# Cross-attention, two layers, one core: rounded spread product, weighted sums two by two, last item behind two shifted steps

## What is computed

```python
# layer 0: queries from x, keys and values from ctx and x together (512 keys)
h = concatenate([ctx, x], axis=1)
q = x @ q_w + q_b;  kmat, v = split(h @ kv_w + kv_b)
attn = softmax(where(mask, q @ kmat.T / DH, -inf))
y = (attn @ v) @ out_w + out_b + x
x1 = gelu(rmsnorm(y) @ w1 + b1) @ w2 + b2 + x
# layer 1: queries from x1, keys and values from the normed ctx (256 keys)
a = layer_norm(ctx);  Q, K, V = x1 @ Wq.T, a @ Wk.T, a @ Wv.T
out = x1 + tanh(gate) * (softmax(Q @ K.T * DH**-0.5) @ V) @ Wo.T
```

## Time and profile before

| what | value |
|---|---|
| median of 3 runs | 2582.08 us (2581.36 to 2582.22) |
| span of the profiled execution | 2577.6 us |
| layer 0's batches | from 52 to 1130 us, 67.3 us each |
| MLP | from about 1140 to 1840 us |
| layer 1's batches | from about 1870 to 2577 us, 43.07 us each |
| PE's granted clock, mean | 0.980 of 2.4 GHz |

### The profile page before, as it was taken

One profiled execution on the slowest core, in us unless ns is written; L12 is line 12 of the kernel. 1 busy time (PEld: TensorE's weight loads), 2 busy tenths in 40 slices (PEclk: granted clock), 3 DMA queues, 4 the chain that ended last, 5 costly groups with the idle time before them and its releaser, 6 DMA issues. The chain is left out here.

```text
span 2577.6 us, 43920 instructions
## 1 busy us (share of the span) xinstructions
PE 2485.2 (96%) x14784; PEld 1931.8 (75%) x14784; DVE 1163.7 (45%) x2222; ACT 1497.8 (58%) x3418; POOL 226.3 (9%) x256
## 2 busy tenths in 40 slices
PE   6999999999999999989999999999899999999998
PEld 5677777777777777658888888888778787877775
DVE  4455555555555555542222122112356565656563
ACT  3777777777777777753222222222267676767675
POOL 1000000000000000010000000000221111121210
PEclk8999999999999999889999999999899999999998
DMA  6433343333444443341111011002244444444442
GB/s 171 100 99 99 98 102 98 97 98 99 106 107 107 107 107 91 91 127 67 50 49 48 1 49 49 30 19 81 82 115 125 121 125 120 126 120 126 119 111 75
DMA packets 148186, 239.00 MB, mean 93 GB/s; under 512 B 25600, under 2 KB 59680, under 8 KB 148144
## 3 DMA queue, kind: packets, MB, share of 16 engines
q1 hardware_dynamic: 148144, 238.46, 34.4%
HBM read 86.28 MB, written 25.21 MB: 43 GB/s over the span
## 5 line engine op out<-in xcount | busy, mean ns | idle before, releaser
L529 ACT ACTIVATE l_score_ps<-l_score_ps,l_neg_max 128x512 f32<-128x512 f32 (+1 forms) x1024 | 567.1, 557 | 291.3 <-DVE l_neg_max L705 289.3
L705 DVE TENSOR_REDUCE l_neg_max<-l_score_ps 128x1 f32<-128x512 f32 (+1 forms) x768 | 490.0, 682 | 69.5 <-PE l_score_ps L942 69.5
L549 ACT ACTIVATE l_probs<-l_score_ps 128x1024 f32<-128x1024 f32 x384 | 386.8, 1018 | 91.8 <-PE l_score_ps L975 89.1
L1239 ACT ACTIVATE mlp_hidden<-mlp_hidden_ps,mlp_b_col 128x512 f32<-128x512 f32 x128 | 88.3, 690 | 495.9 <-PE mlp_hidden_ps L66 495.8
L942 PE MATMUL l_score_ps<-l_stack 97*128 97x512 f32 (+1 forms) x1024 | 319.0, 370 | 27.4 <-ACT l_score_ps L529 12.8
L1274 DVE TENSOR_TENSOR mlp_hidden_l<-mlp_hidden,mlp_hidden_h 128x512 fp32r<-128x512 f32 x128 | 92.9, 725 | 519.3 <-ACT mlp_hidden_h L1241 519.3
L975 PEld LDWEIGHTS l_score_ps<-l_stack 99*128 99x128 f32 x1536 | 211.2, 192 | 116.8 <-issue 90.8
L975 PE MATMUL l_score_ps<-l_stack 99*128 99x256 f32 x1536 | 274.7, 305 | 0.0
L990 PE MATMUL l_o_ps<-l_probs,l_v 128*32 128x256 f32 x3072 | 241.2, 394 | 1.8
L721 DVE TENSOR_TENSOR l_o_norm<-l_o_ps,norm_room 128x256 f32<-128x256 f32 x128 | 54.4, 425 | 387.9 <-PE l_o_ps L990 387.9
L942 PEld LDWEIGHTS l_score_ps<-l_stack 97*128 97x128 f32 x1024 | 175.3, 193 | 71.3 <-ACT l_score_ps L529 40.5
(11 more groups left out here) (133 smaller groups left out, 4308.6 us busy)
## 6 DMA issues: line engine op xcount, KB each, us to landing
l_stack<-room SPq DMA_DIRECT2D x256, 192.0 KB
l_stack<-l_qk SPq DMA_DIRECT2D x256, 128.0 KB
l_stack<-room SPq DMA_DIRECT2D x128, 128.0 KB
l_stack<-l_qk SPq DMA_DIRECT2D x256, 64.0 KB
l_tokens<-in_x SPq DMA_DIRECT2D x16, 512.0 KB, 4.1
l_tokens<-in_ctx SPq DMA_DIRECT2D x16, 512.0 KB, 5.0
l_stack<-room SPq DMA_DIRECT2D x128, 64.0 KB
l_rows<-in_x SPq DMA_DIRECT2D x16, 512.0 KB, 3.4
```

Source lines behind the costliest of these rows:

```text
L529: m = act.activation(e, e, ACT.Exp, bias=neg_max[:, q, h:h + 1], accum_out=row_sum[:, q, h:h + 1])
L549: act.activation(probs[:, s % PROBS, :].rearrange("p (a b) -> p a b", a=2), score_ps[:, 2 * (s % 2):2 * (s % 2) + 2, :], ACT.Exp).then_inc ...
L705: dve.tensor_reduce(out, bank, AXIS_X, ALU.max, negate=True).then_inc(max_done, 1)
L1239: act.activation(hidden[:, m % HBUF, :], hidden_ps[m % 4][:, :], ACT.Gelu_apprx_tanh, bias=b1_col[:, m:m + 1])
```

## The change

Three things, in both layers.

1. The spread becomes a rounded product over the whole array: `shiftT` and `spread` have 128 rows (zeros below) and are float32r; the reciprocal sums are held in a high and a low part (`INV_ROW`, `INV_LOW_ROW`), both of which `spread` picks up. `make_shift` has two more small operations on DVE, `turn_shift` turns 32 columns in place of 24. The set-up on POOL fills two larger tiles and selects twice.
2. The second pass goes by two steps: two shifted, two weigh, with PROBS = 4 and the projections behind the pair.
3. `shifted(a, 0)`, `shifted(a, 1)` and `turn_shift(a, 1)` stand ahead of the last item on PE, and on ACT `exps(a, 0)`, `copy_shift(a, 1)` and `exps(a, 1)` ahead of that item's `high`. The wait for `low_done` stays ahead of the loop. SP's stacks of half 0 wait for at least LOW_WAITED = 5 shifted steps: 5 in place of 4 in layer 1, no change in layer 0.

The DMA scratch of the program is set to 8192, which makes room.

```diff
-    PROBS = 3
+    PROBS = 4
+    LOW_WAITED = 5
...
-    SHIFT_ROWS = INV_ROW + HALF
+    INV_LOW_ROW = INV_ROW + HALF
+    SHIFT_ROWS = INV_LOW_ROW + HALF
...
-        shiftT = sb("shiftT", [SHIFT_ROWS, HALVES, S])
+        inv_raw = sb("inv_raw", [P, QT, HALF])
+        shiftT = sb("shiftT", [P, HALVES, S], F32R)
...
-        spread = sb("spread", [SHIFT_ROWS, GROUPS, P])
+        spread = sb("spread", [P, GROUPS, P], F32R)
...
-                            sp.wait_ge(shifted_done, PSTEPS * a + PSTEPS // HALVES * (half + 1))
+                            sp.wait_ge(shifted_done, PSTEPS * a + max(PSTEPS // HALVES * (half + 1), LOW_WAITED))
...
             def iteration(p, a):
                 for slot in range(SLOTS + 1):
+                    if slot == SLOTS and a is not None:
+                        exps(a, 0)
+                        copy_shift(a, HALVES - 1)
+                        exps(a, 1)
...
                 if a is not None:
-                    for s in range(PSTEPS):
+                    copy_inv(a, 1)
+                    for s in range(2, PSTEPS):
                         exps(a, s)
-                        if s == 1:
-                            copy_inv(a, 1)
...
                 dve.tensor_copy(high.bitcast(F32R), src).then_inc(shift_step, 1)
-                dve.reciprocal(shift[:, half, :, INV_ROW:SHIFT_ROWS], row_sum[:, :, heads])
-                dve.wait_ge(shift_step, HALVES * a + half + 1)
-                dve.tensor_tensor(shift[:, half, :, HALF:2 * HALF].bitcast(F32R), src, high, ALU.subtract
-                                  ).then_inc(shift_made, 1)
+                dve.reciprocal(inv_raw[:, :, :], row_sum[:, :, heads]).then_inc(shift_step, 1)
+                dve.wait_ge(shift_step, 3 * (HALVES * a + half) + 2)
+                dve.tensor_copy(inv_high.bitcast(F32R), inv_raw[:, :, :]).then_inc(shift_step, 1)
+                dve.tensor_tensor(shift[:, half, :, HALF:2 * HALF].bitcast(F32R), src, high, ALU.subtract)
+                dve.wait_ge(shift_step, 3 * (HALVES * a + half) + 3)
+                dve.tensor_tensor(shift[:, half, :, INV_LOW_ROW:SHIFT_ROWS].bitcast(F32R), inv_raw[:, :, :], inv_high,
+                                  ALU.subtract).then_inc(shift_made, 1)
...
+                    if slot == SLOTS - 1 and a is not None:
+                        shifted(a, 0)
+                        shifted(a, 1)
+                        turn_shift(a, HALVES - 1)
...
                 if a is not None:
-                    shifted(a, 0)
-                    shifted(a, 1)
                     spread_sums(a, 1)
                     if p is not None:
                         pe.wait_ge(low_done, ITEMS * (p + 1))
...
-                    for s in range(PSTEPS):
-                        if s + 2 < PSTEPS:
-                            shifted(a, s + 2)
+                    for s in range(0, PSTEPS, 2):
+                        for u in range(s + 2, min(s + 4, PSTEPS)):
+                            shifted(a, u)
                         weigh(a, s)
-                        if s >= KB and s % KB == KB - 1 and s < PSTEPS - 1:
+                        weigh(a, s + 1)
+                        if s >= KB and s % KB == KB - 2 and s < PSTEPS - 2:
                             project(a, s // KB - 1)
```

More of the change, by code:

```diff
@@ L300, in attention_layer @@
         VECTORS = 5 if first else 3
-        CONSTS = 5
+        CONSTS = 7
         def load_tokens(sp, b):
@@ L372, in iteration @@
                                           HALF * half:HALF * (half + 1), Q_COLS]),
-                                shiftT[HALF * part:HALF * (part + 1), half:half + 1, :],
+                                f32(shiftT[HALF * part:HALF * (part + 1), half:half + 1, :]),
                             ).then_inc(shift_loaded[half], 16)
@@ L415, in _ @@
                 pool.wait_ge(ident_made, 2)
[L416 to L423, removed]
+            pool.memset(f32(shiftT[:, :, :]), 0.0).then_inc(const_made, 1)
+            pool.memset(f32(spread[:, :, :]), 0.0).then_inc(const_made, 1)
+            for n, row in enumerate((INV_ROW, INV_LOW_ROW)):
+                pool.wait_ge(const_made, n + 2)
+                by_head = spread[:, :, :].rearrange("p g (j d) -> p g j d", j=HG)
+                pool.affine_select(out=by_head, in_=f32(by_head), compare_op=ALU.not_equal, fill=1.0, base=-row,
+                                   pattern=[[-HG, GROUPS], [-1, HG], [0, DH]], channel_multiplier=1
+                                   ).then_inc(const_made, 1)
+            pool.wait_ge(const_made, 4)
             pool.memset(half_power[:, :], -0.5).then_inc(const_made, 1)
-            pool.wait_ge(const_made, 3)
+            pool.wait_ge(const_made, 5)
             pool.memset(eps[:, :], RMS_EPS if first else LN_EPS).then_inc(const_made, 1)
@@ L534, in copy_shift @@
                 at_least(act, shift_loaded[half], 32 * a)
-                act.activation(shiftT[:, half, :], o_ps[half][0:SHIFT_ROWS, 0:S], ACT.Copy).then_inc(shift_copied, 1)
+                act.activation(shiftT[0:SHIFT_ROWS, half, :], o_ps[half][0:SHIFT_ROWS, 0:S], ACT.Copy).then_inc(shift_copied, 1)
             def copy_inv(a, half):
@@ L578, in iteration @@
                     if a is not None:
-                        for half in range(HALVES):
-                            if TURN_SLOT[half] == slot - 1:
-                                copy_shift(a, half)
+                        if TURN_SLOT[0] == slot - 1:
+                            copy_shift(a, 0)
                         if SPREAD_SLOT == slot - 1:
@@ L711, in make_shift @@
                 src, high = neg_max[:, :, heads], shift[:, half, :, 0:HALF]
+                inv_high = shift[:, half, :, INV_ROW:INV_LOW_ROW]
                 dve.tensor_copy(high.bitcast(F32R), src).then_inc(shift_step, 1)
-                dve.reciprocal(shift[:, half, :, INV_ROW:SHIFT_ROWS], row_sum[:, :, heads])
-                dve.wait_ge(shift_step, HALVES * a + half + 1)
-                dve.tensor_tensor(shift[:, half, :, HALF:2 * HALF].bitcast(F32R), src, high, ALU.subtract
-                                  ).then_inc(shift_made, 1)
+                dve.reciprocal(inv_raw[:, :, :], row_sum[:, :, heads]).then_inc(shift_step, 1)
[5 more added lines that the diff above has]
+                                  ALU.subtract).then_inc(shift_made, 1)
             def normalise(a, g):
@@ L1039, in iteration @@
                         turn_norm(prev)
-                    for half in range(HALVES):
-                        if a is not None and TURN_SLOT[half] == slot:
-                            turn_shift(a, half)
+                    if a is not None and TURN_SLOT[0] == slot:
+                        turn_shift(a, 0)
                     if a is not None and SPREAD_SLOT == slot:
@@ L1391 @@
     from concourse.bass_utils import run_bass_kernel_spmd
-    nc = bacc.Bacc("TRN2", target_bir_lowering=False, num_devices=1)
+    nc = bacc.Bacc("TRN2", target_bir_lowering=False, num_devices=1, dynamic_dma_scratch_size=8192)
     arrays, tensors = {}, {}
```

## The result

The changed kernel takes 2615.19 us (median of 4 runs, 2613.31 to 2616.45) against 2581.85 (4 runs) for the kernel before: ratio 1.0128, 95% interval 1.0113 to 1.0142. It is slower by 33 us; 20 were forecast, and 2612 was the end of the range. The profiled execution has a span of 2614.5, 36.9 more than before's.

A forecast was written before the change was run, and what follows sets the result against it. PE, busy 96% of the span, was taken to bound both layers. Span 2577.6 + 7.5 (layer 0) + 15.7 (layer 1) - 3 (last batches) = 2597.8, plus 4.5 to the median: 2602 us, range 2590 to 2612 (chance 0.57).

The forecast's parts named there:

- Part 1, the spread: Spread of each half: two rounded products replace four fp32 records; 0.8 us saved per half, 0.3 charged for make_shift.
- T0: Start of the third shifted step, shifted(a, 2), the fixed point in each batch from which the forecast counts times.
- Part 2, the pairs: Second pass: a pair takes 2.20 us on average for 2.48; saves 1.7 per layer 0 batch, 1.0 in layer 1.
- Part 3, layer 0: Around the last item: PE waits 2 us for shift rows, 1.7 for low; +0.5 per batch net of pairs.
- Part 3, layer 1: SP's stack string ends 0.9 us later, the ninth score waits 1.8; batch 44.1 for 43.07, +1.05 per batch.
- the signs for both layers: What would show the forecast: among others, PE standing 1.7 us before the third shifted step for low, 30 times.
- Last batches and the first T0: Last batch of each layer, at half clock: -3 us in all (0 to -6); layer 0's fifteen batches each +0.5.
- Around the span: Kernel before's median is 4.5 us above its profiled span; added to the forecast span 2597.8, giving 2602.
- The clock: Rival: PE standing twice for about 2 us per batch halves its clock for some 5 us: 2675 us, chance 0.03.
- Catching up: Rival: the waits let ScalarE's and VectorE's lag drain, so sums and shift rows are ready: 2560 us, chance 0.14.

The follow-up runs named there:

- the first experiment: The changed kernel with SP's string of stack DMAs in layer 1 starting at shifted_done 4 in place of 5 (LOW_WAITED = 4): 2607.99 us.
- Part 3 alone: Kernel before with two shifted steps and the turn ahead of the last item, SP's string from shifted_done 5; fp32 spread, single steps kept: 2714.52 us.
- parts 1 and 2: The changed kernel with the old order put back (rounded spread and pairs kept) and LOW_WAITED 4: 2529.17 us, ratio 0.979 to the kernel before.

## Why the prediction was wrong, point by point

- **Part 1, the spread**: right. 1.05 became 0.24 (two products 0.12 apart), and alone it gives 0.79 per layer 0 batch; for the 0.3 charged for `make_shift` the first spread comes at T0 + 61.15 where it came at T0 + 60.87.
- **Part 2, the pairs**: right. T0 to the third projection 19.66 for the forecast 19.6 in layer 0, and -0.83 in layer 1, where -1.0 was forecast. Luck helped: behind part 3's waits ScalarE has caught up, and alone the part gives 1.40 in place of the 1.7 forecast (19.91, or 20.08 with part 1). The Trainium skill (TensorEngine Tiling (Array Packing), Key Properties) says that a change of tiling mode drains the engine. By the prediction's estimate from it, halving the changes would have gained some 1 us more than the 1.7; the trace shows less than the 1.7, so the rows bear the smaller price.
- **Part 3, layer 0**: right. Waits of 1.80 and 1.68 for 2 and 1.7; +0.59 per ordinary batch for +0.5.
- **Part 3, layer 1**: right. String at T0 + 2.90, ninth score at T0 + 26.92, batch 44.17 for 44.1. The wait at T0 is 1.32, though, not the 1.7 given among the signs for both layers. A number used there, the cost of that wait alone ("1.8 us, and 0.85 on top"), is no measure of what its removal gives: 0.33 per batch, as the first experiment shows.
- **Last batches and the first T0**: the last batches gained 5.2 where 3 were forecast. The first T0 came 2.2 later: part 3's +2.2 with no pairs ahead of it to pay it back, where the sum had it at +0.5 as one of fifteen equal batches. The two errors go opposite ways, and that they nearly cancel is luck.
- **Around the span**: 4.5 us were added, the kernel before's median less its profiled span. The changed kernel's median is only 0.7 above its span, since its profiled run (2616.45) was the longest of the four. That execution took 1.95 more than its span; by the same measure some 2.5 of the 4.5 were only the luck of which execution was profiled. So 3.8 of the distance between the spans doesn't show between the medians.
- **The step that failed** is the rival *The clock*, which was put at nothing in the sum: "In the steady batches the granted clock is 1.00 with waits of up to 1.4 us ... If that came in each batch for some 5 us ... 2675. Chance 0.03." One batch with one wait of 1.41 was taken as proof for two or three waits of 0.75 to 1.94 in each steady batch of both layers. And it was priced as all or nothing; what came is between: nine falls of 1.4 to 2.4 us, 14.4 together. With the slow issues of SP (1.6) these 16.0 are the distance between the forecast span, 2597.8, and the measured one, 2614.5, but for 0.7. Since the clock was left out of the range, the range ended 3 us too early; without the 14.4 the time would have been 2601, near the 2602 forecast.
- **Catching up** is real as a mechanism (ScalarE is ahead after a wait), but nowhere did it pay more than the wait cost.

## What to carry to other kernels

In this kernel a PE that had had no waits paid for new waits of 1.6 to 1.9 us twice: in the wait, and, in some batches, at half clock behind it. So give that case a price between nothing and all, and let the range hold it. Where such a wait can't be removed, products that change nothing can fill it: here 28 us came back from work that is thrown away. Filling one of two such waits moved the falls to the other. And try the parts of a change one by one: two of the three gained 57 us and the third, on top of them, cost 86.

## What the runs showed of the hardware

- The falls don't follow the length or the sum of the waits. In layer 0 of the changed kernel, with waits of 1.80 and 1.68 per batch, the clock fell in 4 of 14 steady batches, and with the 1.68 alone in 3. With the 1.79 alone it fell in 3 where the wait at T0 was filled with products, but in 12 where that wait was gone and the batch 1.4 us shorter. With both filled it fell in none. Each fall cost 1.38 to 1.5 us. Part 3 alone had waits of only 0.97 and 0.86 and a fall in each layer 0 batch, while waits of 1.24 in layer 1 of parts 1 and 2 brought none. Which batch it hits, no run here predicts.
- The Trainium skill (TensorE: Matmul & The Clock Gate, A second HAM failure mode: psum-queue depth-cycling) tells of another kernel in which short idling between groups of products, repeated, makes the clock go up and down and costs throughput, though the median product runs at the full clock. The trace agrees, with 0.59 and 0.62 behind waits of 1.7 to 1.8 us.
- In the profile of part 3 alone (single steps, old spread) the clock stayed down for 20 us with PE busy all the time (0.52); in the pairs of the changed kernel it was up again within two pairs. What makes the difference is open.
- An issue of SP in the string is 0.60 us, but in each profile looked at two or three of the 512 from `qk` took 1.0 to 2.0, nearly all in the first batches of layer 1. In the kernel before one of 1.13 cost nothing and one of 1.83 cost 0.7; in the changed kernel, where the string sets the ninth score, 1.38 and 1.61 in one batch cost some 1.6.
